# A different order of the start-up in a kernel that fuses channel and spatial attention with a quantised FFN

## The reference, cut to what matters

```python
# x: 16 images, 512 channels, 24 x 8 positions (192 tokens an image)
x = x + conv_ref(ln_c(x), fc1_w, fc2_w, sa_w)     # channel gate, then 7x7 spatial gate
t = to_tokens(x)
t = t + ffn_ref(ln_t(t), w1, w2)                  # 512 -> 2048 -> 512
...
def conv_ref(x, fc1_w, fc2_w, sa_w):
    avg, mx = mean(x, (2, 3)), max(x, (2, 3))
    ca = sigmoid(mlp(avg) + mlp(mx))              # mlp: 512 -> 64 -> 512
    x = x * ca[:, :, None, None]
    s = conv7x7(concat([mean(x, 1), max(x, 1)]))
    return x * sigmoid(s)
def bitlinear(x, w):                              # used for w1, then gelu, then w2
    rms = rsqrt(max(mean(w * w), EPS))
    w_quant = clip(round(w * rms), -1, 1) / rms   # weights of -1, 0, 1
    scale = 127 / max(max(abs(x), -1), EPS)
    x_quant = clip(round(x * scale), -128, 127) / scale
    return x_quant @ w_quant.T
```

## Time and profile before

| | us |
|---|---|
| median of 3 runs (304.04 to 304.36) | 304.06 |
| the profiled execution | 304.37 |
| its span, first to last instruction | 302.5 |
| TensorE busy | 264.9 (88%) |
| VectorE busy | 233.7 (77%) |
| ScalarE busy | 228.5 (76%) |
| GpSimd busy | 159.9 (53%) |

### The profile page before, as it was taken

One profiled execution on the slowest core, in us unless ns is written; L12 is line 12 of the kernel. 1 busy time (PEld: TensorE's weight loads), 2 busy tenths in 40 slices (PEclk: granted clock), 3 DMA queues, 4 the chain that ended last, 5 costly groups with the idle time before them and its releaser, 6 DMA issues.

```text
span 302.5 us, 5861 instructions
## 1 busy us (share of the span) xinstructions
PE 264.9 (88%) x1826; PEld 154.4 (51%) x1834; DVE 233.7 (77%) x534; ACT 228.5 (76%) x464; POOL 159.9 (53%) x267
## 2 busy tenths in 40 slices
PE   2556848694999999999999999999999999999994
PEld 2344724372546554655465546554655554444541
DVE  0573669988787898789878988897889787979520
ACT  0873597689488888888888888888888877887541
POOL 8406673616826574647454845485449543556330
PEclk9999975879599999999999999999999999999998
DMA  7999200000535134813580368036803630263855
GB/s 206 371 395 407 81 1 0 2 0 14 58 73 140 34 72 104 223 23 73 125 217 6 72 141 209 0 72 165 187 1 72 173 69 20 55 174 69 132 115 171
DMA packets 71606, 34.20 MB, mean 113 GB/s; under 512 B 52568, under 2 KB 68952, under 8 KB 71064
## 3 DMA queue, kind: packets, MB, share of 16 engines
q1 hardware_dynamic: 69828, 32.78, 43.5%
q10 hardware_dynamic: 1748, 1.05, 1.3%
HBM read 14.94 MB, written 6.29 MB: 70 GB/s over the span
## 4 chain that ended last, share of the span: by engine, by line
PE 49%; DVE 16%; POOL 12%; issue 9%; ACT 8%; ACTq 2%; DMA 1%; another core or an unknown queue 1%; POOLq 1%; DVEq 0%; SPq 0%
PE ps_o L1269 16%; PE ps_h L1256 9%; PE ps_t L1256 8%; POOL v L488 5%; PE front L1186 4%; PE front L1176 3%; POOL rs L482 3%; DVE st L829 3%; POOL w_room L511 3%; PE front L1278 2%; PE small L1202 2%; DVE amax L931 2%; DVE junk_v L966 2%; DVE t L903 2%; ACT junk_p L573 1%
## 5 line engine op out<-in xcount | busy, mean ns | idle before, releaser
L1269 PE MATMUL ps_o<-w2T,hq 128*128 128x512 f16 x368 | 88.8, 379 | 0.3 <-DMA hq<-w_raw 0.3
L511 POOL TENSOR_SCALAR w_room<-w_room,q 128x1024 f32<-128x1024 f32 x48 | 53.6, 1127 | 30.4 <-DVE q L941 29.2
L931 DVE TENSOR_REDUCE amax<-w_room 128x1 f32<-128x1024 f32 (+1 forms) x48 | 57.9, 1207 | 8.7 <-ACT w_room L573 8.7
L1256 PE MATMUL ps_h<-w1T,xq 128*128 128x512 f16 x208 | 55.3, 405 | 1.3 <-ACT xq L573 0.7
L1269 PEld LDWEIGHTS ps_o<-w2T,hq 128*128 128x128 f16 x368 | 35.0, 98 | 33.7 <-DMA hq<-w_raw 0.8
L573 ACT ACTIVATE w_raw<-w_room 128x1024 f16<-128x1024 f16 x46 | 48.4, 1053 | 3.0 <-POOL w_room L511 2.9
L573 ACT ACTIVATE w_room<-ps_h,s 128x512 f32<-128x512 f32 x52 | 35.7, 687 | 12.2 <-PE ps_h L1256 11.7
L1256 PE MATMUL ps_t<-w1T,xq 128*128 128x512 f16 x176 | 42.8, 381 | 0.0
L573 ACT ACTIVATE w_room<-ps_t,s 128x512 f32<-128x512 f32 x44 | 29.5, 689 | 7.0 <-PE ps_t L1256 6.8
L1256 PEld LDWEIGHTS ps_h<-w1T,xq 128*128 128x128 f16 x208 | 19.7, 103 | 23.2 <-issue 4.3
L573 ACT ACTIVATE junk_m<-front 128x192 bf16<-128x192 f32 x64 | 20.5, 328 | 12.4 <-DVE pooled L842 11.7
(11 more groups left out here) (129 smaller groups left out, 468.9 us busy)
## 6 DMA issues: line engine op xcount, KB each, us to landing
out<-w_room SPq DMA_DIRECT2D x15, 384.0 KB, 3.4
x_in<-in_x SPq DMA_DIRECT2D x14, 384.0 KB, 5.2
w_room<-in_L_ffn_w SPq DMA_DIRECT2D x4, 1024.0 KB, 9.1
w_raw<-in_L_ffn_w SPq DMA_DIRECT2D x4, 1024.0 KB, 12.2
x_in<-in_x ACTq DMA_DIRECT2D x2, 384.0 KB, 3.9
hq<-w_raw SPq DMA_TRANSPOSE x48, 3.1
fc_raw<-in_L_conv_fc_w ACTq DMA_DIRECT2D x2, 128.0 KB, 4.3
out<-w_room SPq DMA_DIRECT2D x1, 256.0 KB, 2.3
```

The source lines that it names most:

```text
L511: pool.tensor_scalar(part, part, q2[tile.par][:, 0:1], MAGIC, ALU.mult, ALU.add).then_inc(g_rounded, 1)
L931: chain.mark(dve.tensor_reduce(amax2[:, i:i + 1], w1_room[:, first + i * F // 2:first + (i + 1) * F // 2 + i], AX.X, ALU.max, apply_absolu ...
L1256: last = pe.matmul(banks[b], xq[tile.pair.par][:, tile.s, k, :], w1T[:, k, b * 512:(b + 1) * 512], start=(k == 0), stop=(k == NC - 1))
L1269: last = pe.matmul(out_bank(tile)[:, :], hq[tile.par][:, k, :], w2T[:, k, :], start=(k == 0), stop=(k == NF - 1))
```

## The change

The calls ahead of the loop are put in another order on four engines, and the rounding of w2 is given to GpSimd alone, in passes of half a quarter (1024 columns). In detail: TensorE turns the first two banks of w1 ahead of pair 1's x. Pair 1's statistics and normalisation come after tile 0 of pair 0 has been limited and rounded. Pair 0's tiles 0 and 1 stand earlier in the lists, relative to pair 1's attention, on TensorE and ScalarE. VectorE loses its two quarters of w2. GpSimd rounds the first quarter of w2, then x of tile 1, then the other three. In the first round of the loop, GpSimd's rounding of g of tile 1 is split around the root of the next tile, `ffn_out` gives its first quarter ahead of a turn of v, and the gelu of tile 2 gains a wait for the packing of tile 0's first half.

```diff
-            def round_weights(k, raw):
+            def round_weights(k, raw, quarters):
 
                 pool.wait_ge(w_rms_ready, k + 1)
-                for i in range(4) if k == 0 else (1, 3):
+                for i in quarters:
                     part = quarter(k, raw, i)
-                    pieces = (part[:, 0:2, :], part[:, 2:4, :]) if k == 0 else (part,)
+                    pieces = (part[:, 0:2, :], part[:, 2:4, :]) if k == 0 else (part[:, 0:F // 2], part[:, F // 2:F])
...
             weight_rms(0)
-            round_weights(0, w1_raw)
-            normalise1(Pair(1), 0, 1, 2)
+            round_weights(0, w1_raw, range(4))
             rstd2(Tile(Pair(0), 0))
             round_x(Tile(Pair(0), 0))
+            normalise1(Pair(1), 0, 1, 2)
             weight_rms(1)
-            round_weights(1, w2_raw)
+            round_weights(1, w2_raw, (0,))
             rstd2(Tile(Pair(0), 1))
             round_x(Tile(Pair(0), 1))
-            round_g(Tile(Pair(0), 0))
+            round_weights(1, w2_raw, (1, 2, 3))
             rstd2(Tile(Pair(0), 2))
             round_x(Tile(Pair(0), 2))
-            round_g(Tile(Pair(0), 1))
+            round_g(Tile(Pair(0), 0))
             normalise1(Pair(2), 0, 1, 2)
+            round_g(Tile(Pair(0), 1), (0,))
...
-                body(Pair(c), c < NP - 2, c < NP - 1, c < NP - 3, 0 < c < NP - 2)
+                body(Pair(c), c < NP - 2, c < NP - 1, c < NP - 3, c < NP - 2)
...
+                    elif b == 0 and tile.at() == 2:
+                        wait(act, g16_ready, tile.at(2, -3))
...
             a = spread_ca(Tile(pair0, 2), 0, a)
+            turn_weights(0, w1_raw, (0, 1))
             b = turn_x(Tile(pair1, 0), 1, b)
             a = turn_x(Tile(pair1, 1), 0, a)
-            b = turn_x(Tile(pair1, 2), 1, b)
-            turn_weights(0, w1_raw, (0, 1))
             pe.wait_ge(band_ready, 2)
             conv(pair0)
+            b = turn_x(Tile(pair1, 2), 1, b)
             turn_weights(0, w1_raw, (2, 3, 4, 5, 6, 7))
...
-                ffn_out(Tile(pair, 0), (0, 1))
+                ffn_out(Tile(pair, 0), (0, 1) if pair.c > 0 else (1,))
...
```

More of the change, by code:

```diff
@@ L689, in _ @@
                 sum_channels(Tile(pair0, s))
-            for s in range(NT):
-                copy_x(Tile(pair1, s), (s + 1) % 2)
             act.wait_ge(masks_ready, 2)
-            copy_weights(0, (0, 2))
+            copy_weights(0, (0,))
+            copy_x(Tile(pair1, 0), 1)
+            copy_x(Tile(pair1, 1), 0)
+            copy_weights(0, (2,))
             gate_tokens(pair0)
+            copy_x(Tile(pair1, 2), 1)
             copy_weights(0, (4, 5, 6))
@@ L976, in weight_floor @@
                 dve.tensor_scalar(w_ms[:, k:k + 1], ms_ps[:, k:k + 1], EPS, None, ALU.max).then_inc(w_ms_ready, 1)
[L978 to L983, removed]
             def weight_units(k):
@@ L1058, in _ @@
             row_stats(Tile(pair0, 0))
+            channel_stats(pair1, 0, 1)
             limit(Tile(pair0, 0))
-            token_max(pair1, 0, 1)
+            channel_stats(pair1, 2)
+            aggregate(pair1, 0, 1, 2)
             squares(1, w2_raw, w2_loaded)
             weight_sum(1)
-            token_max(pair1, 1, 1)
+            token_max(pair1, 0, 1)
             weight_floor(1)
-            token_max(pair1, 2, 0)
-            round_weights(1, w2_raw)
-            weight_units(1)
             add_attention(Tile(pair0, 1))
             row_stats(Tile(pair0, 1))
+            token_max(pair1, 1, 0)
+            token_max(pair1, 2, 1)
+            limit(Tile(pair0, 1))
+            token_max(pair1, 3, 0)
             dve.wait_ge(w_turned, 8)
@@ L1072, in _ @@
                 dve.memset(g_eps[i], EPS).then_inc(eps_ready, 1)
-            token_max(pair1, 3, 1)
+            hidden_max(Tile(pair0, 0), 0)
+            weight_units(1)
+            hidden(pair1)
             copy_weights(1, (1,))
-            hidden(pair1)
-            limit(Tile(pair0, 1))
+            hidden_max(Tile(pair0, 0), 1)
+            hidden_scale(Tile(pair0, 0))
             split_gate(pair1)
-            hidden_max(Tile(pair0, 0), 0)
-            copy_weights(1, (5,))
-            scale_channels(Tile(pair1, 0), 1)
-            hidden_max(Tile(pair0, 0), 1)
-            scale_channels(Tile(pair1, 1), 0)
-            hidden_scale(Tile(pair0, 0))
-            scale_channels(Tile(pair1, 2), 1)
             add_attention(Tile(pair0, 2))
             row_stats(Tile(pair0, 2))
+            scale_channels(Tile(pair1, 0), 0)
             limit(Tile(pair0, 2))
+            scale_channels(Tile(pair1, 1), 1)
+            copy_weights(1, (5,))
+            scale_channels(Tile(pair1, 2), 0)
             hidden_max(Tile(pair0, 1), 0)
+            split_stats(pair1)
+            stats1(pair2, 0, 1, 2)
             hidden_max(Tile(pair0, 1), 1)
-            split_stats(pair1)
             hidden_scale(Tile(pair0, 1))
-            channel_stats(pair2, 0, 1, 2)
             sum_conv(pair1)
-            aggregate(pair2, 0, 1, 2)
             def body(pair, attend, normalise, turn):
@@ L1363, in _ @@
+            ffn_in(Tile(pair0, 0), h_start, (0, 1))
             b = turn_v1(pair1, 0, 1, b)
-            a = turn_xq(Tile(pair0, 0), 0, a)
-            ffn_in(Tile(pair0, 0), h_start, (0,))
-            b = turn_v1(pair1, 1, 1, b)
-            a = turn_v1(pair1, 2, 0, a)
             weight_mean(1)
-            ffn_in(Tile(pair0, 0), h_start, (1,))
             ffn_in(Tile(pair0, 0), h_start, (2,))
-            b = turn_v1(pair1, 3, 1, b)
+            a = turn_v1(pair1, 1, 0, a)
             ffn_in(Tile(pair0, 0), h_start, (3,))
-            turn_weights(1, w2_raw, (0, 1, 2))
+            b = turn_v1(pair1, 2, 1, b)
@@ L1374, in _ @@
+            a = turn_v1(pair1, 3, 0, a)
+            turn_weights(1, w2_raw, (0, 1))
+            b = turn_xq(Tile(pair0, 1), 1, b)
             fc1(pair1)
+            turn_weights(1, w2_raw, (2,))
+            fc2(pair1)
+            ffn_in(Tile(pair0, 1), h_start, (0,))
             turn_weights(1, w2_raw, (3,))
-            fc2(pair1)
+            turn_ca(pair1)
+            ffn_in(Tile(pair0, 1), h_start, (1,))
             turn_weights(1, w2_raw, (4,))
-            a = turn_xq(Tile(pair0, 1), 0, a)
+            a = spread_ca(Tile(pair1, 0), 0, a)
@@ L1379, in _ @@
+            b = spread_ca(Tile(pair1, 1), 1, b)
+            ffn_in(Tile(pair0, 1), h_start, (2,))
+            a = spread_ca(Tile(pair1, 2), 0, a)
             turn_weights(1, w2_raw, (5,))
-            turn_ca(pair1)
+            ffn_in(Tile(pair0, 1), h_start, (3,))
+            b = turn_x(Tile(pair2, 0), 1, b)
             turn_weights(1, w2_raw, (6,))
-            b = spread_ca(Tile(pair1, 0), 1, b)
-            a = spread_ca(Tile(pair1, 1), 0, a)
+            a = turn_x(Tile(pair2, 1), 0, a)
@@ L1407, in body @@
                     a = turn_res(Tile(pair.plus(-1), 2), OUT_BANK[0], a)
+                if pair.c == 0:
+                    ffn_out(Tile(pair, 0), (0,))
                 if attend:
                     b = turn_v1(att, 0, V1_BANK[0], b)
-                ffn_out(Tile(pair, 0), (0, 1))
+                ffn_out(Tile(pair, 0), (0, 1) if pair.c > 0 else (1,))
                 if attend:
```

59 lines of the change are left out of this document (25 added, 34 removed).

## The result

The median of four runs is 309.0 us (307.87 to 310.45) against 304.06: the ratio is 1.0148, with a 95% interval of 1.0115 to 1.0181. (The ratios are as recorded; the quotient of these two medians is 1.016.) Six more runs of the unaltered change, with 23 of the kernel before on the same chip, give 309.62 against 305.3, ratio 1.0141 (1.0107 to 1.0174). The profiled execution of the change took 310.45, 6.08 more than that of before.

What follows compares the result with a forecast made beforehand. TensorE is busy 29.34 of each 29.76 us round, so lateness at the loop's entrance reaches the end. Lateness 6.25 less 0.55 for the clock gives 5.7, on 304.37 310.1, less 0.31: 309.8 us; range 304.0 to 312.0.

Steps and rivals of the forecast that it cites:

- w1's turns ahead of x's: Start-up: copies of w1's banks run without a gap, so tile 0's first product starts at 44.42, a gain of 1.4 us.
- The squares block GpSimd: Pair 1's normalisation: VectorE's two-operand squares of w2 hold GpSimd until 51.4; TensorE waits 3.5 us, w2's root 3.4 late.
- the squares don't block: Rival at pair 1's normalisation: it ends at 47.0, later moments come 3.5 us earlier, 306.3 us; chance 0.20.
- GpSimd alone rounds w2: Before the gate: two passes end at 56.7, six follow tile 1's rounding from 60.9 and end at 68.35.
- The gate behind the passes: Pair 1's gate on VectorE: each of three steps waits for a GpSimd pass; ends at 68.5 against 63.51, 5.0 late.
- the sign: At pair 1's gate: its three VectorE steps taking over 2 us would show the prediction right.
- From the gate to the loop: Chain from the gate's end to the loop's first product: that product starts at 84.0, 5.6 us late.
- the loop's first stretch: From the loop's first product to the next pair's: late pair 2 statistics and normalisation put xq at 95.35, 6.2 us late.
- The clock: Tile 1's second block and neighbours, reckoned at 1.2 GHz, could save 1.65 us at 2.4 GHz; 0.55 taken off the sum.
- Faster: Rival throughout the start-up: VectorE and GpSimd hardly hold each other up, 301.3 us; decided at the gate; chance 0.12.
- no change: Rival at the loop's entrance: pair 0's tiles fill TensorE so the later gate stays off its path, 304.1 us; chance 0.08.

Runs made afterwards that it cites:

- passes held: The changed kernel with GpSimd's last four passes over w2 held back until pair 1's gate is split: 308.29 us, ratio to before 1.0100.
- gate ahead: The changed kernel with pair 1's gate steps moved ahead of VectorE's second hidden maximum and the two small steps behind it: 309.87 us, ratio to before 1.0165.
- limit behind: The changed kernel with VectorE's limit of tile 2 moved behind the third scaling of pair 1's channels: 305.75 us, ratio to before 1.0039.
- one operand: The changed kernel with VectorE's two squares of w2 replaced by sums of absolute values, one SBUF operand each, nothing moved: 305.08 us, ratio to before 0.9996.
- the change once more: The changed kernel run again unaltered, six runs: 309.62 us, ratio to before 1.0141.
- the order of before: The kernel before, its order kept, with GpSimd alone rounding all of w2 in eight passes: 304.43 us, ratio to before 0.9998.
- squares away: The changed kernel with w2's squares taken out of VectorE's stretch behind pair 1's statistics, ScalarE squaring three quarters: 305.53 us, ratio to before 1.0012.
- three edits: The changed kernel with w2's squares moved away, GpSimd's last four passes held until the gate is split, tile 2's limit behind the third scaling: 301.78 us, ratio 0.9915.
- the extra work: The changed kernel with 16 extra transposes on TensorE between 26 and 33 us, its band-matrix wait moved earlier: 309.17 us, ratio to before 1.0151.
- the fourth edit: GpSimd rounds tile 0's hidden values ahead of tile 2's x, added to the kernel with three edits: 302.5 us, ratio to before 0.9926.

## Why the prediction was right

The forecast was 309.8 and the result 309.0. The mechanism held: the squares blocked GpSimd, TensorE stood behind that, and the gate met GpSimd's passes. That the single times fit so closely is in part luck, since several terms were wrong in opposite directions. By its own steps:

*w1's turns ahead of x's, 1.4 us.* In the profiled execution the first product came at 45.18, a gain of 0.7. There TensorE turned two banks of w1 in 1.91 us from 34.65 on. In three kernels that are the same up to that place (passes held, gate ahead, limit behind) the x16 took 1.06 and the product came at 44.42 to 44.55, which is the 44.42 reckoned. In two more profiles the x16 took 1.91 and 1.92, and the product came at 45.59 (one operand) and 46.27 (the change once more), the last of them 0.4 later than before's 45.86. So the term was right for three of six profiles; in the others it was 0.7, 0.3 and -0.4.

*The squares block GpSimd.* This was chosen without a row and is now shown: normalised at 52.09 (51.4 reckoned, and the first product was 0.76 late), a TensorE wait of 3.77 (3.5), the root at 53.78 (53.9). The root's start fits by chance: its input was ready at 53.70 and not at 53.1, and the add, which I had put ahead of the root at 0.75, began at 53.61 and shows in the root's own length, 0.98 where it took 0.55 before. The one-operand run gives the lock a price of 4.5 us in the time. The rival "the squares don't block" is refuted. The Trainium skill's rule (SBUF — State Buffer, section Who interferes with whom) is that a VectorE instruction with two SBUF inputs contends with a GpSimd instruction that reads SBUF, and that one with at most one SBUF input does not, outside VectorE's 2-port modes, which take the shared ports too. The trace agrees: 2.41 and 2.25 us beside the squares, 0.27 and 0.19 beside the sums. The number of inputs alone doesn't decide, though: the gate's first step has one and took 0.62 beside the passes. Whether it ran in such a mode no run here shows.

*GpSimd alone rounds w2.* Six passes from 61.15 to 67.92 (60.9 to 68.35 reckoned). They took 6.77 us, so VectorE's steps among them, for which I had added 0.85, hardly lengthened them: VectorE waited for the passes, and they hardly for it. Its cost is only where it falls: none in the order of before.

*The gate behind the passes, 5.0 us late.* It ended at 68.13 (68.5), 4.6 late. Two steps waited where I had three, and they took 1.9 us where over 2 was to be the sign; in exchange the hidden layer's second step, reckoned without a wait, took 1.07. The price of that collision alone is small, 1.3 us in the time and hardly clear of noise. When the squares are away the gate ends at 63.94, 0.4 later than before, with its passes still beside it, so most of its lateness was handed down from the squares.

*From the gate to the loop, and the loop's first stretch.* 83.95 (84.0) and 95.15 (95.35). The working had the limit of tile 2 ahead of the second scaling and added up right, but it did not say that this place is itself a cost of the change. The run with the limit behind shows that it costs about 1%, three quarters of what the squares cost. The prediction would have been better for naming it, since before had paid for the same stretch in other ways: 14.9 us then, 15.8 with the change, 11.8 with the limit behind.

*The clock, -0.55.* Tile 1's second block took 1.91 us and its third 1.03, so the full loss at that block fell due, and the loop's entrance did not show the allowance. Nor was the reason the one given: TensorE idled 1.65 us ahead of the gate's turn and not 3.7, and the eight turns of w2 ahead of that idle time already took 1.06 us, against 0.61 for eight at 72.94. In the profiled pair the difference is 6.05 at the loop's next pair and 6.08 in the time, against 5.7 forecast. The medians differ by 4.3 to 4.9 only, since the profiled execution of the change was the slowest of its four.

*Faster, and no change.* The first was to be decided at the gate, ahead of 63 within 1 us; it ended at 68.13 after 1.9 us. The lists weren't so well filled that the gate stayed off the path. What the rival "faster" needed, no blocking, does give a faster kernel when the order supplies it: 301.78, near its 301.3, though by another road.

## What to carry to other kernels

Where two engines lock each other out, look for the pairs that a new order brings together, not at how busy each engine is: here two steps of 0.2 to 0.3 us, each held by a 2.3 us operation with two SBUF operands, cost 4.5 us, because an in-order queue stood behind them. Replacing the long operation in its place by one with a single SBUF operand tells the lock from the order, which moving it elsewhere does not. A wait for data in one list (here a limit in the midst of three scalings) can cost nearly as much as the lock, and the gains from undoing several collisions need not add: three edits gave 3.9, 1.3 and 3.1 us apart, and 6.9 together.

## What the runs showed of the hardware that was not expected

The gate's three VectorE steps among back-to-back GpSimd passes advanced by one pass for each step: moved ahead, they took 0.60, 1.05 and 1.06 us and ended with the passes, and the move gained nothing. Not every small step is held so: those of 128x1 just ahead of the gate took 0.21 and 0.17 among the same passes.

TensorE's turns at 34.6 us took 1.06 or 1.91 us for the same 16 in kernels that are the same up to there. For two of them the granted clock of the window 34.6 to 36.5 goes with it, 0.50 and 1.00, the lower and the upper level; the columns are length, busy us (instructions) by engine, the clock, and the DMA's share and GB/s. First the change, then the kernel with held passes:

```profile
34.60:36.50 1.90, 1.90 (x18) 1.65 (x15) 0.00 (x0) 0.75 (x1) 0.47 (x1) 0.50 0.00 0
```

```profile
34.60:36.50 1.90, 1.05 (x19) 0.91 (x18) 0.84 (x2) 1.32 (x3) 0.59 (x1) 1.00 0.00 0
```

It doesn't always: in the kernel with the squares away and in the change's second profile the x16 took 1.91 and 1.92 us, and the clock over them read 1.00. The profiled executions of the change with 1.9 us were the slowest of their runs (310.45 and 311.4), those of the held passes, the gate ahead and the extra work, with 1.06, the fastest of theirs (307.78, 308.49, 307.74); but with the limit behind, 1.06 went with 305.58, and with one operand, 1.91 went with 304.99, both in the midst of their runs, and with the fourth edit 1.06 went with 303.42, the second slowest of six. That the level there makes the spread was not tried, and stays open.
